# Output weights times the inverse-value product: both halves of the array rows crossed to both halves of the columns, in a transformer layer on one core

## What is computed

```python
out = attn1 @ attn2_inv @ (attn3 @ v)          # 1024x64 @ 64x64 @ 64x64 for each batch and head
res = conv(out, w_conv)                        # 13 taps along the rows, one filter per head
out = out + res
out = out.transpose(0, 2, 1, 3).reshape(b, n, H * DH)
out = out @ w_fc + b_fc                        # 1024 @ 256
x = x + out                                    # then layer norm, router, experts
```

## Time and profile before

| what | value |
|---|---|
| median of 3 runs | 1206.57 us |
| the profiled execution, its own time | 1203.91 us |
| its span | 1202.2 us |
| mean granted TensorE clock | 0.983 of full speed |
| TensorE matmul busy | 1127.5 us, 94% of the span |
| VectorE busy | 612.3 us, 51% |
| ScalarE busy | 300.8 us, 25% |
| POOL busy | 303.7 us, 25% |
| landmark stage (8 rounds) | about 409 to 435.7 us in the span |
| row stage | 435.7 to about 764 us |
| expert stage | 799 us to the end |

### The profile page before, as it was taken

One profiled execution on the slowest core, in us unless ns is written; L12 is line 12 of the kernel. 1 busy time (PEld: TensorE's weight loads), 2 busy tenths in 40 slices (PEclk: granted clock), 3 DMA queues, 4 the chain that ended last, 5 costly groups with the idle time before them and its releaser, 6 DMA issues.

```text
span 1202.2 us, 24795 instructions
## 1 busy us (share of the span) xinstructions
PE 1127.5 (94%) x9834; PEld 912.8 (76%) x9834; DVE 612.3 (51%) x1283; ACT 300.8 (25%) x535; POOL 303.7 (25%) x297
## 2 busy tenths in 40 slices
PE   3999999999988899999999999649999999999997
PEld 3767667676677756677767767549999999999996
DVE  7354342233267466676686677654444444444442
ACT  4432222222233322332333233211111111111110
POOL 5000000000010003235534553524322323224332
PEclk9999999999999999999999999769999999999999
DMA  9300000000110030211322222333232232322321
GB/s 341 122 1 1 1 1 1 1 1 1 54 40 5 3 140 19 103 56 63 134 75 79 68 95 69 112 107 46 48 50 46 47 49 46 50 47 43 48 44 12
DMA packets 48704, 68.19 MB, mean 57 GB/s; under 512 B 8272, under 2 KB 42192, under 8 KB 47568
## 3 DMA queue, kind: packets, MB, share of 16 engines
q1 hardware_dynamic: 34288, 45.92, 12.1%
q0 software_dynamic: 13296, 16.92, 8.2%
q10 hardware_dynamic: 1008, 3.78, 0.8%
HBM read 41.05 MB, written 26.46 MB: 56 GB/s over the span
## 4 chain that ended last, share of the span: by engine, by line
PE 90%; DVE 3%; issue 3%; POOL 1%; ACT 1%; DMA 1%; POOLq 0%; SPq 0%; DVEq 0%; ACTq 0%
PE ps L1458 21%; PE ps L1468 10%; PE ps L1360 10%; PE ps L1158 9%; PE ps L1138 9%; PE ps L1399 9%; PE ps L1391 5%; PE ps L1149 3%; PE ps L1272 2%; PE ps L1379 1%; PE ps L1452 1%; PE ps L1101 1%; PE ps L1345 1%; PE ps L1113 1%; PE ps L1256 1%
## 5 line engine op out<-in xcount | busy, mean ns | idle before, releaser
L1458 PEld LDWEIGHTS ps<-mem 128*128 128x128 f32 x2272 | 266.6, 193 | 4.5 <-DVE mem L1067 0.9
L1458 PE MATMUL ps<-mem 128*128 128x128 f32 x2272 | 267.2, 276 | 0.6 <-ACT mem L697 0.6
L508 POOL DMA_INDIRECT out<-mem x71 | 126.4, 1780 | 278.6 <-DVE mem L1061 201.7
L1468 PE MATMUL ps<-mem 128*128 x568 | 134.5, 380 | 0.9 <-DVE mem L1080 0.9
L463 POOL TENSOR_TENSOR mem<-mem,small 128x1024 f32<-128x1024 f32 x36 | 68.5, 1904 | 248.7 <-DVE small L986 115.6
L1360 PE MATMUL ps<-mem 128*128 128x512 f32 x288 | 129.7, 594 | 1.3 <-DVE mem L870 1.3
L705 ACT ACTIVATE mem<-ps 128x512 f32<-128x512 f32 x71 | 42.4, 598 | 326.4 <-PE ps L1458 326.4
L1399 PE MATMUL ps<-mem 128*128 128x256 f32 x512 | 120.7, 390 | 0.0
L1138 PE MATMUL ps<-mem 128*128 128x512 f32 x256 | 115.4, 593 | 0.0
L1158 PE MATMUL ps<-mem 128*128 128x256 f32 x512 | 113.2, 379 | 0.9 <-DVE mem L762 0.9
L1158 PEld LDWEIGHTS ps<-mem 128*128 128x128 f32 x512 | 97.2, 190 | 20.7 <-issue 7.2
(11 more groups left out here) (198 smaller groups left out, 1286.1 us busy)
## 6 DMA issues: line engine op xcount, KB each, us to landing
mem<-xs_d SPq DMA_DIRECT2D x71, 130.0 KB, 2.1
mem<-w_gu SPq DMA_DIRECT2D x8, 1024.0 KB, 5.8
mem<-x SPq DMA_DIRECT2D x8, 512.0 KB, 7.8
mem<-x SPq DMA_DIRECT2D x32, 128.0 KB, 2.2
out<-mem SPq DMA_DIRECT2D x32, 128.0 KB, 1.7
mem<-w_down SPq DMA_DIRECT2D x8, 512.0 KB, 5.8
xnt_d<-mem ACTq DMA_DIRECT2D x3, 1056.0 KB, 5.7
mem<-xnt_d SPq DMA_DIRECT2D x3, 1056.0 KB, 4.9
```

The lines of the kernel that those rows point to most:

```text
L508: pool.indirect_dma_start(out=out_rows, out_offset=bass.IndirectOffsetOnAxis(ap=xs[:, v, D + 1:D + 2].bitcast(U32), axis=0), in_=ys[:, v], ...
L1458: mm = pe.matmul(bank(2 * c + u)[:, f * P:(f + 1) * P], wgu[:, u, k, c, f * P:(f + 1) * P], xst[:, u, k], start=(k == 0), stop=(k == KD - 1))
L1468: mm = pe.matmul(bank(4 + u)[:, 0:D], hid[:, u, f * P:(f + 1) * P], w_d_s[:, e, f], start=(f == 0), stop=(f == 3))
```

## The change

Of the four pairs of a round in the landmark stage, the second and fourth (i odd) now write crossed: the even head's matmul writes the upper half of the PSUM partitions and the odd head's the lower half. They go to the second bank of the two, while the first and third pair stay straight in the first bank. VectorE's copy puts the two banks back into the order of the pairs in `pm`. In the row stage the convolution writes the heads of every second pair to the other halves, so that they meet the rows of `pm`: the halves for heads 0, 1, 2, 3, 4, ... were 0, 1, 0, 1, 0, ... and are now 0, 1, 1, 0, 0, 1, 1, 0, and so on.

```diff
                 dve.wait_ge(s("p_mm"), g + 1)
-                dve.tensor_copy(pm[:, g // 2, 4 * (g % 2):4 * (g % 2) + 4],
-                                bank(2 + 2 * (g % 2), 2).rearrange("p (s c) -> p s c", s=4)).then_inc(s("p_pm"), 1)
+                dve.tensor_copy(pm[:, g // 2, 4 * (g % 2):4 * (g % 2) + 4].rearrange("p (s o) c -> p o s c", o=2),
+                                bank(2 + 2 * (g % 2), 2).rearrange("p (o s c) -> p o s c", o=2, s=2)).then_inc(s("p_pm"), 1)
...
                 for i in range(4):
                     q = 4 * g + i
-                    for r in halves:
-                        mm = pe.matmul(bank(2 + 2 * (g % 2), 2)[r, i * D:(i + 1) * D], wts[r, g % 2, i], wfc[r, q % J],
-                                       start=True, stop=True)
+                    to = bank(2 + 2 * (g % 2) + i % 2)[:, i // 2 * D:(i // 2 + 1) * D]
+                    for h, r in enumerate(halves):
+                        mm = pe.matmul(to[halves[(h + i) % 2]], wts[r, g % 2, i], wfc[r, q % J], start=True, stop=True)
                 mm.then_inc(s("p_mm"), 1)
...
                 for h in range(H):
-                    c = 64 * (h % 2)
+                    c = 64 * ((h + h // 2) % 2)
                     mm = pe.matmul(bank(4, 2)[c:c + 64, (h // 2) * P:(h // 2) * P + TO], a1[:, q % 2, h], band[:, h],
                                    start=True, stop=True)
```

## The result

| | before | changed |
|---|---|---|
| median | 1206.57 us (5 runs, 1205.54 to 1208.38) | 1199.6 us (5 runs, 1198.47 to 1201.0) |
| ratio | | 0.9943, 95% interval 0.9931 to 0.9956 |
| profiled execution, own time | 1203.91 us | 1199.60 us |
| its span | 1202.2 us | 1197.9 us |

What follows compares the result with a forecast made beforehand. TensorE was taken as the bound, its matmuls busy 94% of the span. The product's -6.9 us, all else costed at nothing, gave 1199.7 us from the median 1206.57 us; range 1197.0 to 1203.3 us.

Steps and rivals of the forecast that it cites:

- The pace of four quadrants: Landmark stage's product: four quadrants at full pace save 0.86 us per round, 6.9 us in 8; loss at most 0.7 us.
- Rival A: Landmark product: two quadrants on the same rows take turns, so the time stays at 1206.6 us; chance 0.07.
- half-way form: Landmark product: quadrants run at three quarters of their pace, saving 3.4 us and ending near 1203 us.
- the rule of the Trainium skill on weight loads: Landmark product: a weight load overlaps running matmuls only for another row group; 16 loads would add 1.06 us a round.
- What ends a round: Landmark rounds: TensorE's round falls from 3.40 to 2.54 us, nothing new is late, VectorE keeps 0.3 us of slack.
- The warning of the Trainium skill: Landmark rounds: packing speeds matmuls but not PSUM copies, which can become the bottleneck; VectorE's 1.99 us stays below 2.54 us.
- Rival C: Landmark stage: the copy becomes the bound above 1.7 us; at 2.0 us per copy, 1203.1 us; chance 0.04.
- The convolution's order: Row stage: the new order of halves (0, 1, 1, 0) costs nothing, a tile stays at 1.81 us.
- Rival B: Row stage convolution: the order costs slots; strict program order gives 1228 us, two lost slots per tile 7.1 us; chance 0.06.
- The sum: Whole kernel: 6.9 us less, a median of 1199.7 us against 1206.57 us, 0.57% less.
- The 2 us each way that were kept for the clock: Expert stage: starting at another moment, its half-speed clock phase may cost 2 us less or more; likeliest no change.

Runs made afterwards that it cites:

- experiment 1: The changed kernel run again without any edit: 1198.45 us, ratio 0.9932 to the kernel before.
- experiment 2: The changed kernel with the convolution's old order of halves (0, 1, 0, 1), product still crossed: 1198.53 us, ratio 0.9934 to the kernel before.
- experiment 10: The changed kernel once more without any edit, in a later group of runs: 1198.23 us, ratio 0.9951 to the kernel before.
- experiment 3: The kernel before with only the convolution's new order of halves, product straight as before: 1204.98 us, ratio 0.9991 to the kernel before.
- experiment 5: The changed kernel with a round's pairs issued 0, 2, 1, 3, straight passes first, then crossed: 1198.91 us, ratio 0.9952 to the kernel before.
- experiment 6: The kernel before with the convolution's heads issued in runs of four on one column half: 1222.15 us, ratio 1.0144 to the kernel before.
- experiment 7: The kernel before with the convolution's heads issued in runs of eight, all even then all odd: 1247.41 us, ratio 1.0349 to the kernel before.
- experiment 9: The kernel before with the convolution's heads issued in runs of three on one column half: 1212.16 us, ratio 1.0071 to the kernel before.
- experiment 4: The kernel before with all four pairs of a round crossed, so still two quadrants work: 1202.88 us, ratio 0.9969 to the kernel before.

## Why the prediction was right

- *The pace of four quadrants.* Forecast 0.86 us less per round, with up to 0.7 us in all kept back for a loss. The round went from 3.40 to 2.54 us, the stage lost 6.87 us, the same in three further profiles of the unedited product (experiments 1, 2 and 10), and the loss is not to be seen. The reading that carried it, one engine 95% busy yet with two of four quadrants empty, came from setting the pace of single passes against the time of the group. Rival A, with its half-way form, falls by the 1.09 us and by the busy sum. So does the rule of the Trainium skill on weight loads that the prediction set beside it (TensorE: Matmul & The Clock Gate, Part 3, The mechanism): the trace does not agree with it, since 16 loads of 132 ns lie within 0.64 us, and eight of them in one row half, one after the other, would alone be 1.06 us.
- *What ends a round.* VectorE's slack was forecast at 0.3 us ahead of L863, and is 0.27 us in the round shown. The warning of the Trainium skill (TensorEngine Tiling (Array Packing), PSUM Bottleneck) points at the engine that came nearest: VectorE's idle time fell from 1.42 to 0.56 us in a round, and the copies did not become the bound. Rival C falls with the copy's 1224 ns.
- *The convolution's order.* Costed at nothing, and experiment 3 measured nothing. The reason that I gave, a pass that began ahead of four older ones, was too general, though. What counts is not how many older passes wait but how many wait for the same half: six in two quadrants are fine (experiment 5), a fourth in one is not (experiments 6, 7 and 9). The four older ones of the earlier trace rows lay in two quadrants, two in each. That is just the two that the change needs, not twice as many, as the prediction had it. There is one to spare all the same: worked slot by slot with 99 ns a slot, an estimate, the change's order would lose nothing with two waiting passes and 0.4 us per tile with one, because its first run is only one head long and the halves are staggered from there on. With three waiting the same working gives the last starts of experiments 6, 7 and 9 to within 5 ns. Rival B in its strict form falls by experiment 3, but a milder form of it is real: it had reckoned that two lost slots per tile eat the gain, and a tile that begins with three heads on one half loses two and a half of them and costs 8.0 us, more than the change brings.
- *The sum.* 6.9 us forecast; 7.0 us by the medians, and 7.9, 7.8, 5.9 and 5.9 us in experiments 1, 2, 5 and 10, of which 2 and 5 are variants. With a scatter of a microsecond either way, that the first median came within 0.1 us of the forecast is luck; the 6.87 us of the stage are not. The 2 us each way that were kept for the clock were not drawn on by the medians. In the profiled pair the clock took 0.83 us, and two longer waits, which the prediction had no term for, took 1.14 and 0.43 us.

## What to carry to other kernels

A busy matmul engine can be half empty: set the time of a group against the number of its passes times the pace of one, and where two of four quadrants work, sending every second matmul to the other half of the PSUM partitions and to another bank nearly halves the group (1.95 to 1.09 us here), as long as the copies out of PSUM fit in what remains. Whether the other bank is needed was not tested: no run has straight and crossed matmuls write the same bank together. Then look at the order: alternate the quadrants so that never more than four passes (two float32 matmuls) in a row go to the same one; such a run was free even where it stood first (experiment 5). Groups of different quadrants also fill each other up across group bounds, for 2.8 us of the stage here with the same count and shapes of matmuls (experiment 4, which leaves out the matching order of the convolution, so that its result is not the reference's).

## What the runs showed of the hardware

- Passes start out of program order across quadrants, and every start in experiments 4 to 7 and 9 fits a limit of three waiting passes per quadrant or column half (or of one waiting matmul of two passes). A half that has run dry pays 150 ns for its first slot of 116 columns, 99 ns after that; the first slot of every tile is 150 ns as well.
- Four quadrants with 256 moving columns each run at the full pace of 0.216 us a pass (0.266 us for the first one in each), two of them reading the same 64 partitions of SBUF, and two of them writing the same PSUM partitions in different banks.
- A copy of 1024 elements out of PSUM takes 1224 or 1225 ns whether its pattern is plain or in four pieces with a swapped order.
